# A four-stage sequence kernel: score products over 32 rows, and the inverse's products over 128 rows with 64 weight columns

## The reference, cut to what matters

```
# delta rule, per head (8 heads, keys of 128, values of 64), step by step over 512 tokens
retained = einsum('bhvk,bhk->bhv', state, k_t)
rk = retained[..., None] * k_t[:, :, None, :]
vk = v_t[..., None] * k_t[:, :, None, :]
state = a4 * (state - b4 * rk) + b4 * vk
o_t = einsum('bhvk,bhk->bhv', state, q_t)

# select, per sequence: the 256 tokens with the highest gate attend to each other, 16 heads of 16
_, idx = top_k(gate, C)
attn_in = take_along_axis(token_inputs, idx[..., None], axis=1)
scores = einsum('bqhd,bkhd->bhqk', q, k) / sqrt(dh)
attn = softmax(scores, axis=-1)
o = einsum('bhqk,bkhd->bqhd', attn, v).reshape(B, C, D) @ Wo
```

## Time and profile before

| | us |
|---|---|
| median of 3 runs | 3659.09 (3657.68 to 3662.07) |
| the profiled execution | 3664.74 |
| its span, first to last instruction | 3662.9 |
| PE busy | 3098.5 (85%) |
| PE weight loads busy | 2337.5 (64%) |
| DVE busy | 2386.8 (65%) |
| ACT busy | 1272.0 (35%) |
| POOL busy | 172.6 (5%) |

### The profile page before, as it was taken

How to read it: one execution, slowest core, us unless ns; L and a number is a source line. 1 busy time by engine, 2 the same in 40 slices (tenths; PEclk the granted TensorE clock), 3 DMA queues, 4 the chain that set the end, 5 groups by cost and what they waited for, 6 DMA issues and landing times. The chain is left out here.

```text
span 3662.9 us, 47688 instructions
## 1 busy us (share of the span) xinstructions
PE 3098.5 (85%) x17546; PEld 2337.5 (64%) x17546; DVE 2386.8 (65%) x5793; ACT 1272.0 (35%) x2465; POOL 172.6 (5%) x165
## 2 busy tenths in 40 slices
PE   5999946898999999964889789798989888488887
PEld 2655534454899999942566667676767677355654
DVE  6787624554677777775677878686877774354442
ACT  2333201221344444422444444434344431123322
POOL 0000000006111111100000000000000000000000
PEclk8999967999999999986888889797979875678886
DMA  1000081003599989963011011111101100100000
GB/s 65 21 14 18 12 155 24 12 1 136 208 318 320 321 320 321 320 233 106 27 36 36 36 36 39 33 59 35 45 35 39 36 15 1 61 12 24 12 18 12
DMA packets 203643, 326.78 MB, mean 89 GB/s; under 512 B 37449, under 2 KB 157522, under 8 KB 202258
## 3 DMA queue, kind: packets, MB, share of 16 engines
q1 hardware_dynamic: 196930, 305.97, 25.2%
q0 software_dynamic: 6480, 17.77, 1.3%
HBM read 275.18 MB, written 48.50 MB: 88 GB/s over the span
## 5 line engine op out<-in xcount | busy, mean ns | idle before, releaser
L767 PE MATMUL ex_ps<-ex_xbT,ex_w 128*128 128x128 f32 x4544 | 530.3, 275 | 0.5 <-issue 0.5
L767 PEld LDWEIGHTS ex_ps<-ex_xbT,ex_w 128*128 128x128 f32 x4544 | 524.0, 192 | 4.3 <-issue 0.7
L1386 PE MATMUL de_ps<-de_hT,de_w 128*128 128x512 f32 x640 | 321.9, 649 | 23.7 <-DMA de_w<-in_w_kqv_dram 18.6
L896 ACT ACTIVATE ex_t<-ex_ps,ex_b 128x128 f32<-128x128 f32 x568 | 208.5, 367 | 334.7 <-PE ex_ps L767 305.8
L711 PE MATMUL ex_ps<-ex_xT,ex_w 128*128 128x512 f32 x512 | 229.8, 605 | 12.5 <-DVE ex_gl L1008 9.1
L1386 PEld LDWEIGHTS de_ps<-de_hT,de_w 128*128 128x128 f32 x640 | 126.3, 208 | 154.0 <-issue 146.4
L1008 DVE SCALAR_TENSOR_TENSOR ex_gl<-ex_ps,ex_b,ex_t 128x128 f32<-128x128 f32 (+1 forms) x316 | 123.7, 392 | 136.5 <-ACT ex_t L896 69.6
L711 PEld LDWEIGHTS ex_ps<-ex_xT,ex_w 128*128 128x128 f32 x512 | 97.7, 194 | 131.6 <-issue 114.8
L1577 PE MATMUL de_ps<-de_qx,de_kx 128*128 128x128 f32 x512 | 77.0, 316 | 98.0 <-ACT de_qx L1644 98.0
L1822 DVE SCALAR_TENSOR_TENSOR de_ya<-de_qx,de_taps,de_ya 128x512 f32<-128x512 f32 x192 | 141.4, 750 | 18.8 <-ACT de_ya L1632 14.0
L1822 DVE SCALAR_TENSOR_TENSOR de_ya<-de_kx,de_taps,de_ya 128x512 f32<-128x512 f32 x192 | 143.5, 749 | 15.4 <-ACT de_ya L1632 10.8
(11 more groups left out here) (380 smaller groups left out, 5975.0 us busy)
## 6 DMA issues: line engine op xcount, KB each, us to landing
ex_w<-in_w_all_dram SPq DMA_DIRECT2D x144, 1024.0 KB, 6.3
ex_w<-in_w_all_dram SPq DMA_DIRECT2D x72, 512.0 KB, 8.7
de_w<-in_w_kqv_dram SPq DMA_DIRECT2D x80, 256.0 KB, 3.2
de_ab<-alpha_d SPq DMA_DIRECT2D x8, 2048.0 KB, 7.1
ex_xb<-ex_xs_d SPq DMA_DIRECT2D x71, 129.0 KB
ex_xs_d<-ex_blank SPq DMA_DIRECT2D x71, 128.5 KB, 8.4
ex_w<-ex_y_d SPq DMA_DIRECT2D x16, 512.0 KB, 6.2
mx_xin<-in_x_dram SPq DMA_DIRECT2D x8, 512.0 KB, 3.9
```

Source lines behind the costliest of these rows:

```text
L767: m = pe.matmul(ps[:, n % 4, x * BLK:(x + 1) * BLK], w[:, k, part * HID + c * P:part * HID + (c + 1) * P], xbT[sx][:, k, :], start=(k == 0 ...
L896: act.activation(t1[:, n % 2, 0:BLK], ps[:, n % 4, 0:BLK], ACT.Identity, bias=b13[s][:, 0, n:n + 1]).then_inc(t1_ready, 1)
L1386: m = pe.matmul(ps[:, n % 2, :], w[:, g % SLOTS, k, n % 2 * P:(n % 2 + 1) * P], hT[:, k, :], start=(k == 0), stop=(k == KT - 1))
```

## The change

In the delta stage, x5 streams 64 columns instead of 32: the block of its own head and that of the next one, whose result lands in columns that nobody reads (for the last head the block before it is taken instead, 32 columns further left). y6 takes all 128 rows of DG, but only its right 64 columns as weights, and all 128 rows of X11, whose lower half is zero; the result goes straight to the lower 64 partitions of PSUM. x6 takes all 128 rows of Y6, whose upper half is zero, and of XT. POOL clears the two halves once per sequence, after ACT's `spread_left`, and PE waits for that (semaphore `rest`) before the first y6. In the select stage the score products take all 32 rows of a head.

```diff
                     for hd in range(H):
-                        m = pe.matmul(ps[0:HALF, 4 + c % 2, hd * Q:(hd + 1) * Q], Y5[:, c % 2, hd, :], XTd[:, c * H + hd, :],
+                        n = c * H + hd
+                        back = 1 if n == BL - 1 else 0
+                        col = hd * HALF - back * Q
+                        m = pe.matmul(ps[0:HALF, 4 + c % 2, col:col + HALF], Y5[:, c % 2, hd, :],
+                                      XTd[:, n - back:n - back + 2, :].rearrange("p a b -> p (a b)"),
                                       start=True, stop=True, skip_group_check=True)
...
-                        m = pe.matmul(ps[:, 2 + c % 2, hd * HALF:(hd + 1) * HALF], DG[0:HALF, c, hd, :], X11[0:HALF, c % 2, hd, :],
+                        m = pe.matmul(ps[HALF:P, 2 + c % 2, hd * HALF:(hd + 1) * HALF], DG[:, c, hd, HALF:P], X11[:, c % 2, hd, :],
...
-                        m = pe.matmul(ps[0:HALF, 4 + c % 2, hd * HALF:(hd + 1) * HALF], Y6[HALF:P, c % 2, hd, :], XT[HALF:P, c, hd, HALF:P],
+                        m = pe.matmul(ps[0:HALF, 4 + c % 2, hd * HALF:(hd + 1) * HALF], Y6[:, c % 2, hd, :], XT[:, c, hd, HALF:P],
...
-                x11(0), x11(1), y6(0), y6(1), x6(0), x6(1)
+                x11(0), x11(1)
+                pe.wait_ge(s["rest"], 2 * b + 2)
+                y6(0), y6(1), x6(0), x6(1)
...
-                                           ps[lo * Q:(lo + 1) * Q, 4 + c % 2, 0:H * Q].rearrange("p (h t) -> p h t", t=Q), ACT.Copy)
+                                           heads(4 + c % 2)[lo * Q:(lo + 1) * Q, :, 0:Q], ACT.Copy)
...
                 pool.memset(Xc, 0.0).then_inc(s["xz"], 1)
+                pool.wait_ge(s["xc"], b + 1)
+                pool.memset(X11[HALF:P, :, :, :], 0.0).then_inc(s["rest"], 1)
+                pool.memset(Y6[0:HALF, :, :, :], 0.0).then_inc(s["rest"], 1)
...
-        rows = lambda i: slice(i * PAD, i * PAD + KROWS)
+        rows = lambda i: slice(i * PAD, (i + 1) * PAD)
```

More of the change, by code:

```diff
@@ L1278, in stage_delta @@
         names = ("loaded zeroed folded w0 w1 w2 hT_ld bg_ld ab_ld cl_ld x_ld out_st "
-                 "pj up ks qs su os gk ktp y5p x5p x11p nrow nqt y6p x6p vtp nqm gq oTp opp "
+                 "pj up ks qs su os gk ktp y5p x5p rest x11p nrow nqt y6p x6p vtp nqm gq oTp opp "
                  "cp tap u ktr dd xc xt x5 x11 x6 sq sqo oTr "
@@ L2062, in stage_select @@
     NQ = H // QUAD
-    KROWS = DH + 1
     SCALE = DH ** -0.5
```

## The result

The changed kernel takes 3532.33 us (median of 4 runs, 3528.49 to 3537.61) against 3658.51 before. The ratio is 0.9654, 95% interval 0.9638 to 0.9671: 127 us less where 122 were forecast. The profiled execution has a span of 3535.8 us.

A forecast was written before the change was run, and what follows sets the result against it. PE, running at half clock while busy, was taken to be late in the delta inversions, with DVE's convolutions following it. Inversion 95 us (41 from y6's price included) plus scores 27 make 122: 3659.1 - 122 = 3537 us, range 3500 to 3605.

The forecast's parts named there:

- Price of a matmul: Delta inversion: weight columns set the price; with 64 of them, 62 ns at full clock and 112 at half.
- parts 1 and 2: Delta inversion: x5 streaming 64 columns instead of 32 costs nothing; y6 with 64 weight columns saves 41 us.
- Part 2: Delta inversion: y6 over 128 rows with 64 weight columns, at unchanged clock, saves 5.1 us per inversion, 41 us.
- rival D: Both stages: clock levels don't answer to rows and stay; only y6's cheaper matmuls gain, 41 us, 3618 us; chance 0.07.
- Rival B: Delta inversion: columns count too, so y6 and x6 don't keep the clock up; 68 us in all, 3591; chance 0.15.
- Part 3: Delta inversion: clock stays 1.00 from x5 to last x6; first-y6-to-last stretch 17.0 us instead of 28.9, 95 us in all.
- The sign that I had named: Delta inversion: key-query products starting 11 to 12 us sooner after the first y5.
- the choice: Delta inversion: clock falls because few array rows are fed; feeding 128 rows, weights no wider than stream, keeps it at 1.00.
- Part 4: Delta stage: POOL's two memsets per sequence, about 2 us, are hidden by 8 us before PE needs them.
- Part 5: Select stage: scores over 32 rows raise the clock earlier, 2.9 us per step, 27 us in sum.
- rival E: Select stage: score matmuls filling their row groups stop overlapping, 168 us more, 3705 us; chance 0.05.

The follow-up runs named there:

- the narrow kernel: Kernel before the change with only y6 altered, 64 weight columns instead of 128, still over 64 rows: 3572.97 us, ratio 0.9772.
- The run over few rows: Kernel before the change with y6 at 64 weight columns, and y6 and x6 over 32 rows, half of each sum left out: 3600.74 us, ratio 0.9841.
- y5 in pieces: Changed kernel with each y5 matmul split into two products of 32 weight and 32 moving columns: 3480.48 us, ratio 0.952.
- the scan: All scan products cut into four pieces of 32 weight columns, on top of y5 in pieces: 3419.28 us, ratio 0.9341.
- the x5 pieces: x5, y6 and x6 also cut into pieces of 32 weight columns, on top of y5 in pieces: 3474.44 us, ratio 0.9487.

## Why the prediction was right

**Price of a matmul, parts 1 and 2.** 62 ns were taken for 64 weight columns at full clock; y6 has 1.90/32 = 59 and x6 2.01/32 = 63. Wider x5 costs nothing. Part 2 by itself, 41 us at an unchanged clock, is the one term that no run shows: the narrow y6 alone brings 84 us by its ratio, because it also keeps the clock, and over 32 rows, where the clock falls later than before, 58. Rivals D and B, at 41 us and 68, were priced with it.

**Part 3.** The stretch is 16.7 us in seven inversions (17.0 forecast) and 13.3 in the last, where I had feared 5 us more; 231.5 - 130.3 = 101 us against 95. The 6 us between them are mostly a slip of mine: the last inversion has no projections, so two times 1.9 us should have been left out of its 17.

The convolutions behind the stretch did follow: the key-query product starts 2319.42 - 2282.96 = 36.5 us after the first y6, where it was 2368.10 - 2320.13 = 48.0, 11.5 us sooner. The sign that I had named was 11 to 12 us sooner after the first y5. That came in four of the eight inversions. In the other four it is 14 to 17 us: in the fourth and fifth, half-clock time had reached into the first y5 too (the fourth's took 5.23 us, now 3.79), and in the first, the fifth and the last the stretch itself had been longer than in the others, 30 us against 28. So from first y5 to key-query product the eight together win 109 us, more than forecast, and the stage wins 98: some 12 us are lost again between a key-query product and the next sequence's first y5 (109.7 us behind the fourth, where it was 108.2). What is late there was not looked into, and that the stage came within 3 us of the forecast owes something to these two cancelling.

The direction of the choice held, that rows count and busy time does not. Its reason was incomplete. I named two things that the change does, all rows fed and "no more columns of weights than of stream", but gave the fall to the first, "few rows of the array fed", and expected later, for the narrow kernel, that 64 rows would let the clock fall again. They don't, when they are fed densely and the clock is up already. The sum survived because the change does both things at once.

The rule that was weighed there, of the Trainium skill (TensorE: Matmul & The Clock Gate, Part 1, "What's actually happening"), is that the clock follows how busy PE has been. It was counted as rival D, 3618 us. The run over few rows is against it as a rule for this kernel: PE busy 3.88 of 3.88 us in y6 and x6, and behind them 0.50. So is the narrow kernel's last inversion, busy 22.81 of 22.81 us at 0.50. Here the measurement decides.

**Part 4.** The two memsets take 0.95 and 0.94 us and start with y5, at 2272.14; y6 starts at 2282.96. They are hidden by 8.9 us (8 forecast), and no idle time of PE before y6 is ended by POOL (it is ACT, 0.33).

```profile
2272.14 0.95 POOL L1809 MEMSET de_PQ<- 64x1024 f32 x1 [50.30 <-ACT de_vb L1686]
2273.14 0.94 POOL L1810 MEMSET de_PQ<- 64x1024 f32 x1
```

**Part 5.** The two wide groups take 3.72 us each, and the step is 3371.24 - 3316.63 = 54.6 us, as forecast, where it was 58. Here is that step, with one group of turned scores (L2178), and then the kernel's last group, which took 5.94:

```profile
3316.63 1.16 PE L2161 MATMUL se_ps<-se_kT,se_qT 32*128 32x256 f32 x16
...
3338.97 3.72 PE L2218 MATMUL se_ps<-se_psel,se_h 128*128 128x256 f32 x16
...
3343.86 1.16 PE L2178 MATMUL se_ps<-se_q,se_kT 32*128 32x256 f32 x16 [0.51 <-DVE se_q L2401]
3344.95 1.07 PE L2188 MATMUL se_ps<-se_PT,se_V 128*32 128x256 f32 x16
...
3352.76 3.72 PE L2234 MATMUL se_ps<-se_selT,se_wq 128*128 128x256 f32 x16
...
3371.24 1.16 PE L2161 MATMUL se_ps<-se_kT,se_qT 32*128 32x256 f32 x16
```

```profile
3527.05 3.72 PE L2272 MATMUL se_ps<-se_o,se_pselT 128*128 128x256 f32 x16 [0.69 <-ACT se_o L2359]
```

The scores overlap as before over 32 rows (16 in 1.09 us), which rules out rival E. Rival B, that 64 of 128 columns count as half the work and y6 and x6 would therefore not keep the clock up, has the 1.00 of all eight stretches against it, and of seven in the narrow kernel, which feeds only 64 rows as well.

## What to carry to other kernels

Where PE is busy and its granted clock is low, look at how many rows of the array its matmuls feed and whether the weight load is longer than the stream; filling the rows with zeros, or loading only the weight columns whose result is read, kept the clock up here at no cost of its own. Where the clock was already down, in the last inversion, only the kernels with all 128 rows brought it back. A product with few moving columns is priced by its weight columns, and cut into pieces of 32 weight columns that write to different groups of 32 PSUM partitions it can cost less than whole. Take such an edit apart before explaining it: here two reasons stood in one line of code, and in seven of eight inversions either was enough.

## What the runs showed of the hardware that I had not expected

- Matmuls of 32 weight columns over all 128 rows, written to different column groups, overlap: 18 ns each with two groups and 32 moving columns, 29 to 30 with two groups and 64, and 16 with four groups and 64 (14 where another group of such pieces follows). A matmul of 128 weight columns and 64 moving columns takes 108 ns, four pieces that do the same work 65.
- Two stretches with the same matmul lengths and no gap left the clock at different levels: y6 and x6 over 64 rows, 1.00; over 32 rows, 0.50 behind them.
- Rows of zeros count as fed: y6 and x6 over a zero half at 1.00, and scores over 15 padded rows with 29 us less in their stage.
- A stretch that holds the full clock need not bring it back: the narrow y6 over 64 rows kept 1.00 in seven inversions and stayed at 0.50 for 22.8 us in the eighth.
- Less half-clock time is not always less time: from 24 rows to 32 the select stage lost about 40 us of it and 4 us of its length, and PE's wait for DVE's maxima grew by 9 us.

Open is where 13 of the 57 us of y5 in pieces come from, and whether the scan and the x5 pieces together would go below 3419 us; that was not tried.
